# Full 128x128 stationary operands for the attention of a fused LayerNorm, attention and routed-FFN kernel on eight cores

## The reference

```python
mask = (ki <= qi) & ((qi - ki < WINDOW) | (ki < PERSIST))      # 128, 16
attn = softmax(where(mask, q @ k.T * hd**-0.5, min))
x + (attn @ v) @ Wo + ffn(xn)
```

## Time and profile before

| what | value |
|---|---|
| median of 3 runs | 5688.84 us |
| lowest and highest of the 3 | 5360.26 and 5897.46 us |
| the profiled execution | 5357.17 us |
| its span, slowest core | 5355.5 us |
| spans of the eight cores | 5347.5 to 5355.5 us |
| granted TensorE clock, mean of each core | 0.996 to 0.998 |
| PE busy, of the span | 98% |
| DVE, ACT, POOL busy | 28%, 20%, 5% |
| first scores, start of periods 0 and 7 | 3745.3 and 5161.7 us |

### The profile page before, as it was taken

One profiled execution on the slowest core, in us unless ns is written; L12 is line 12 of the kernel. 1 busy time (PEld: TensorE's weight loads), 2 busy tenths in 40 slices (PEclk: granted clock), 3 DMA queues, 4 the chain that ended last, 5 costly groups with the idle time before them and its releaser, 6 DMA issues.

```text
span 5355.5 us, 77837 instructions; the slowest of 8 cores (5347.5 to 5355.5 us)
## 1 busy us (share of the span) xinstructions
PE 5274.2 (98%) x27655; PEld 2478.0 (46%) x27655; DVE 1498.3 (28%) x3547; ACT 1083.1 (20%) x2801; POOL 253.4 (5%) x369
## 2 busy tenths in 40 slices
PE   6999999999999999999999999999999999999998
PEld 3444444444444444444444444444444444444444
DVE  3201013310111431102123010112555445454454
ACT  3010110101001010010100101001544344344343
POOL 1111011000000000000000000000000000000000
PEclk9999999999999999999999999999999999999999
DMA  9777779733342753343272222236254563654546
GB/s 224 152 152 151 172 157 225 192 97 90 90 110 79 236 130 98 99 99 103 93 253 79 79 79 71 72 126 228 95 170 134 168 191 115 183 179 134 165 135 196
DMA packets 255857, 749.90 MB, mean 140 GB/s; under 512 B 20416, under 2 KB 109056, under 8 KB 248320
## 3 DMA queue, kind: packets, MB, share of 16 engines
q1 hardware_dynamic: 130784, 482.74, 27.0%
q0 software_dynamic: 117984, 216.04, 20.4%
q10 hardware_dynamic: 6720, 46.14, 2.7%
HBM read 684.03 MB, written 174.06 MB: 160 GB/s over the span
## 4 chain that ended last, share of the span: by engine, by line
PE 96%; DMA 2%; issue 1%; DVE 0%; ACT 0%; SPq 0%; POOL 0%; ACTq 0%; DVEq 0%; POOLq 0%
PE ps L453 33%; PE ps L467 32%; PE ps L487 11%; PE ps L512 8%; PE ps L502 2%; PE ps L495 2%; PE ps L565 1%; PE ps L547 1%; PE ps L568 1%; DMA ring<-w 1%; DMA ring<-wt 1%; PE ps L545 1%; DMA acc<-x 1%; PE ps L546 1%; PE ps L532 1%
## 5 line engine op out<-in xcount | busy, mean ns | idle before, releaser
L453 PE MATMUL ps<-xnT,ring 128*128 128x512 bf16 x8192 | 1779.9, 380 | 11.1 <-DMA ring<-wt 5.7
L467 PE MATMUL ps<-ring,hT 128*128 128x512 bf16 x8192 | 1777.6, 379 | 4.5 <-DMA ring<-w 4.5
L453 PEld LDWEIGHTS ps<-xnT,ring 128*128 128x128 bf16 x8192 | 802.5, 98 | 982.3 <-issue 22.4
L467 PEld LDWEIGHTS ps<-ring,hT 128*128 128x128 bf16 x8192 | 801.0, 98 | 968.0 <-issue 9.3
L681 DVE SCALAR_TENSOR_TENSOR acc<-ps,gcol,acc 128x512 f32<-128x512 f32 x512 | 384.2, 750 | 2627.6 <-PE ps L467 2627.3
L832 ACT ACTIVATE hT<-ps,b1T 128x512 bf16<-128x512 f32 x512 | 351.7, 687 | 3113.8 <-PE ps L453 3113.0
L487 PE MATMUL ps<-xnT,ring 128*128 128x512 bf16 x2560 | 591.0, 380 | 0.1
L512 PE MATMUL ps<-ring,qT 128*128 128x512 bf16 x2048 | 478.1, 382 | 2.4 <-DMA ring<-wt 2.4
L932 ACT COPY pT_sb<-ps 128x384 bf16<-128x384 bf16 x512 | 244.6, 478 | 658.3 <-PE ps L547 646.9
L487 PEld LDWEIGHTS ps<-xnT,ring 128*128 128x128 bf16 x2560 | 232.6, 98 | 265.0 <-issue 0.2
L924 ACT ACTIVATE p_sb<-ps,negmax 128x272 bf16<-128x272 f32 x512 | 252.5, 493 | 218.1 <-DVE negmax L759 218.0
(11 more groups left out here) (82 smaller groups left out, 2435.4 us busy)
## 6 DMA issues: line engine op xcount, KB each, us to landing
ring<-wt SPq DMA_DIRECT2D x752, 512.0 KB, 5.6
ring<-w POOLq DMA_DIRECT2D x128, 512.0 KB, 12.8
wt<-ring SPq DMA_DIRECT2D x128, 512.0 KB, 6.9
acc_d<-acc POOLq DMA_DIRECT2D x16, 2048.0 KB, 16.6
base<-acc_d POOLq DMA_DIRECT2D x64, 512.0 KB, 10.7
y<-base POOLq DMA_DIRECT2D x64, 512.0 KB, 9.4
xln<-x ACTq DMA_DIRECT2D x24, 1024.0 KB, 9.2
acc<-x POOLq DMA_DIRECT2D x12, 2048.0 KB, 22.8
```

The lines of the kernel that those rows point to most:

```text
L453: i = e.matmul(bank(g)[:], w[:, cc, jj * 128:(jj + 1) * 128], xnT2[:, half, c, :], start=(c == 0), stop=(c == 15))
L467: i = e.matmul(bank(g)[:], hT[:, c, s * 128:(s + 1) * 128], w[:, cc, :], start=(c == 0), stop=(c == 15))
```

## The change

All stationary operands of the attention become 128x128.

- `p_sb` grows from 272 to 384 columns; DVE writes zeros to columns 256 to 383 of its four buffers at the program's start (four memsets, counted by `v_set`), and the exponent and the normalisation still write the columns up to 271. The third transpose takes columns 256 to 383.
- `vper` grows from 16 to 128 rows. POOL fills both buffers with zeros before the attention stage, and `persist` waits for that (`g_zero`) and writes its 16 rows. The third values product takes all 128 rows.
- The two scores matmuls of 128 moving columns become one of 256 where the slots `a` and `b` lie next to each other in `kbuf` (five of six cases).
- For t = 0 the part before and the first keys are left out, and for t = 1 the first keys: in scores, transposes, values products, and in the columns that `mask`, `row_max`, `exponent`, `normalize` and `copy_pT` touch.
- The memsets of `kbuf` and `vbuf` on POOL, the memset of `ps_p` on DVE, and the waits of PE on them are gone.

```diff
...
     rinv = [A("rinv%d" % j, [128, 1], F32, o + 8480 + 32 * j) for j in range(4)]
-    p_sb = [A("p_sb%d" % j, [128, 272], BF16, o + 8608 + 576 * j) for j in range(4)]
-    pT_sb = [A("pT_sb%d" % j, [128, 384], BF16, o + 10912 + 768 * j) for j in range(2)]
-    stg_bf = A("stg_bf", [16, 128], BF16, o + 12448)
-    stg_f32 = A("stg_f32", [64, 128], F32, o + 12704)
-    o += 13248
+    p_sb = [A("p_sb%d" % j, [128, 384], BF16, o + 8608 + 768 * j) for j in range(4)]
+    pT_sb = [A("pT_sb%d" % j, [128, 384], BF16, o + 11680 + 768 * j) for j in range(2)]
+    stg_bf = A("stg_bf", [16, 128], BF16, o + 13216)
+    stg_f32 = A("stg_f32", [64, 128], F32, o + 13472)
+    o += 14016
...
     qT = [A("qT0", [128, H, BLK], BF16, o_ln), A("qT1", [128, H, BLK], BF16, o_acc)]
-    vper = [A("vper%d" % j, [16, Dm], BF16, o_ln + 16384 + 4096 * j) for j in range(2)]
+    vper = [A("vper%d" % j, [128, Dm], BF16, o_ln + 16384 + 4096 * j) for j in range(2)]
     vbuf = A("vbuf", [128, KS, Dm], BF16, o_acc + 16384)
...
     d_id, d_b1, d_mask, d_small = sem("d_id"), sem("d_b1"), sem("d_mask"), sem("d_small")
-    v_set, v_zero, g_zero = sem("v_set"), sem("v_zero"), sem("g_zero")
+    v_set, g_zero = sem("v_set"), sem("g_zero")
...
         return n % KS
+
+    def window(it):
+
+        t = it // NIT % BPB * NS + it % NIT // H
+        return t >= 1, t >= 2
+
+    def columns(it):
+        back, first = window(it)
+        return slice(0 if back else 128, 272 if first else 256)
...
                 wait_ffn_evicted(e, 4 + b2)
-                e.wait_ge(g_zero, 1)
+            back, first = window(it)
             q = qT[m % 2][:, h, s * 128:(s + 1) * 128]
             a, b = slot_k(m * NS + s + KS - 1), slot_k(m * NS + s)
-            e.matmul(ps_s[b2][:, 0:128], q, kbuf[:, a, h, :], start=True, stop=True)
-            e.matmul(ps_s[b2][:, 128:256], q, kbuf[:, b, h, :], start=True, stop=True)
-            e.matmul(ps_s[b2][:, 256:272], q, kper[m // BPB][:, h, :],
-                     start=True, stop=True).then_inc(t_sc, 1)
+            ps = ps_s[b2]
+            if back and a < b:
+                i = e.matmul(ps[:, 0:256].rearrange("p (s n) -> p s n", n=128), q,
+                             kbuf[:, a:b + 1, h, :], start=True, stop=True)
+            else:
+                if back:
+                    e.matmul(ps[:, 0:128], q, kbuf[:, a, h, :], start=True, stop=True)
+                i = e.matmul(ps[:, 128:256], q, kbuf[:, b, h, :], start=True, stop=True)
+            if first:
+                i = e.matmul(ps[:, 256:272], q, kper[m // BPB][:, h, :],
+                             start=True, stop=True)
+            i.then_inc(t_sc, 1)
...
             else:
-                e.wait_ge(v_zero, 1)
+                wait_ffn_evicted(e, 6)
+            back, first = window(it)
             pT = as_bf(ps_p)
-            e.transpose(pT[:, 0:128], p_sb[b4][:, 0:128], id_bf[:])
-            e.transpose(pT[:, 128:256], p_sb[b4][:, 128:256], id_bf[:])
-            e.transpose(pT[0:16, 256:384], p_sb[b4][:, 256:272],
-                        id_bf[:]).then_inc(t_pT, 1)
+            for c in [0] * back + [1] + [2] * first:
+                i = e.transpose(pT[:, c * 128:(c + 1) * 128],
+                                p_sb[b4][:, c * 128:(c + 1) * 128], id_bf[:])
+            i.then_inc(t_pT, 1)
...
                 wait_ffn_evicted(e, 7)
-                e.wait_ge(g_zero, 2)
+            back, first = window(it)
             p = pT_sb[it % 2]
-            a, b = slot_k(m * NS + s + KS - 1), slot_k(m * NS + s)
             hs = slice(h * 128, (h + 1) * 128)
-            e.matmul(ps_o[:, 0:128], vbuf[:, a, hs], p[:, 0:128], start=True, stop=False)
-            e.matmul(ps_o[:, 0:128], vbuf[:, b, hs], p[:, 128:256],
-                     start=False, stop=False)
-            e.matmul(ps_o[:, 0:128], vper[m // BPB][:, hs], p[0:16, 256:384],
-                     start=False, stop=True).then_inc(t_av, 1)
+            keys = [vbuf[:, slot_k(m * NS + s + KS - 1), hs], vbuf[:, slot_k(m * NS + s), hs],
+                    vper[m // BPB][:, hs]]
+            seen = [0] * back + [1] + [2] * first
+            for c in seen:
+                i = e.matmul(ps_o[:, 0:128], keys[c], p[:, c * 128:(c + 1) * 128],
+                             start=(c == seen[0]), stop=(c == seen[-1]))
+            i.then_inc(t_av, 1)
...
         e.memset(mhalf[:], -0.5).then_inc(v_set, 1)
+        for j in range(4):
+            e.memset(p_sb[j][:, 256:384], 0.0).then_inc(v_set, 1)
         n_bn = 0
...
             wait_evicted(e, ("v", b * BPB, 3, NS - 1))
-            e.tensor_copy(vper[b][:], vbuf[0:PER, sk, :]).then_inc(v_per, 1)
+            e.wait_ge(g_zero, 2)
+            e.tensor_copy(vper[b][0:PER, :], vbuf[0:PER, sk, :]).then_inc(v_per, 1)
         def mask(it):
             m, s = it // NIT, it % NIT // H
             t = (m % BPB) * NS + s
+            cols = columns(it)
             ps = ps_s[it % 2]
             e.wait_ge(t_sc, it + 1)
-            e.tensor_tensor(ps[:, 0:272], ps[:, 0:272], masks_sb[:, min(t, 2), :],
+            e.tensor_tensor(ps[:, cols], ps[:, cols], masks_sb[:, min(t, 2), cols],
                             ALU.add).then_inc(v_msk, 1)
         def row_max(it):
             e.wait_ge(v_msk, it + 1)
-            e.reduce_max(negmax[it % 4][:], ps_s[it % 2][:, 0:272], axis=AX.X,
+            e.reduce_max(negmax[it % 4][:], ps_s[it % 2][:, columns(it)], axis=AX.X,
                          negate=True).then_inc(v_max, 1)
...
             e.wait_ge(v_inv, it + 1)
-            e.tensor_scalar(p_sb[b4][:], p_sb[b4][:], rinv[b4][:], None,
-                            ALU.mult).then_inc(v_p, 1)
-
-        wait_ffn_evicted(e, 6)
-        e.memset(ps_p[:, 128:192], 0.0).then_inc(v_zero, 1)
+            p = p_sb[b4][:, columns(it)]
+            e.tensor_scalar(p, p, rinv[b4][:], None, ALU.mult).then_inc(v_p, 1)
+
         e.wait_ge(d_mask, 48)
...
                 e.wait_ge(t_pT, it - 3)
-            e.activation(out=p_sb[b4][:], in_=ps_s[it % 2][:, 0:272], func=AF.Exp,
+            cols = columns(it)
+            if it < 4:
+                e.wait_ge(v_set, 6)
+            e.activation(out=p_sb[b4][:, cols], in_=ps_s[it % 2][:, cols], func=AF.Exp,
                          bias=negmax[b4][:],
...
                 e.wait_ge(t_av, it - 1)
-            e.copy(pT_sb[it % 2][:], as_bf(ps_p)[:, 0:384]).then_inc(a_pT, 1)
+            back, first = window(it)
+            cols = slice(0 if back else 128, 384 if first else 256)
+            e.copy(pT_sb[it % 2][:, cols], as_bf(ps_p)[:, cols]).then_inc(a_pT, 1)
...
-        e.wait_ge(t_d, P.ffn_units)
-        e.memset(kbuf[:, KS - 1, :, :], 0.0).then_inc(g_zero, 1)
+        for b in range(BPC):
+            e.memset(vper[b][:], 0.0).then_inc(g_zero, 1)
         for sl in range(4):
             e.wait_ge(st_acc[sl], 16 * NFB)
-        e.memset(vbuf[:, KS - 1, :], 0.0).then_inc(g_zero, 1)
```

## The result

Against the kernel before, on the same chips, the ratio of times is 0.9626, with an interval of 0.961 to 0.9642: 3.7% faster. The changed kernel's median of 5 runs is 5160.9 us, the shortest 5153.65; the profiled execution takes 5159.94. The shortest of before is 5358.29. Some executions of either kernel are longer since the cores of one die or of both are granted a lower clock (in the changed kernel's 5950.69 us, cores 4 to 7 have 0.852 to 0.857 where cores 0 to 3 have 0.995 to 0.998, and in a later execution of the kernel before, of 5820.25 us, 0.912 to 0.915); the ratios leave them out, but medians of few runs are moved by them, so that 5688.84 against 5160.9 isn't what the change did.

A forecast was written before the change was run, and what follows sets the result against it. PE was taken as the bound, busy for 98% of the span. Savings of 202 + 1 + 14 less 11 and 8 gave 198, taken as 200 us: 5157 us from 5357.17, 8-in-10 range 5130 to 5217.

The forecast's parts named there:

- Part 1: Attention slots: third transpose and third values product full size, small steps 0.056 us each; saves 0.394 us per slot, 202 us.
- The bound of 0.07 for a full step: Transposes and values products: largest step seen between two full operands, putting the six between 0.33 and 0.42 us.
- Part 2: Scores: one product of 256 columns takes 0.109 us against 0.112 for two of 128; saves 1 us in all.
- Part 3: Items with t = 0 and t = 1: skipped parts save 10 us and 4.5 us, together 14 us.
- Part 4: Gains given back as PE waits: 11 us for the probabilities in short slots, 8 us for key banks.
- key banks: Slots with three key units: ACT evicts after its copy of the transposed probabilities, so PE waits for banks; 8 us lost.
- Part 5: Moved memsets on POOL and DVE, loads of `base`, and PE's new wait for the bank of `ps_p`: costed at nothing.
- One padding alone: Rival: only one of the two paddings helps, part 1 gives 96 us less; 5241 us, 6%.
- Had the size not been the cause: Rival: operand size doesn't cause the long steps, they stay and only the skips gain, 38 us; 5319 us, 3%.
- The slots of 8 matmuls: Rival: the probabilities' way bounds these slots, 2.40 us instead of 2.21, giving back 60 us; 5217 us, 6%.
- The slower rival: PE's waits bring the clock to 1.2 GHz in periods 0, 4 and 7, costing 409 us; 5566 us, 2%.
- The step that failed: Whole execution: 5157 us forecast against the profiled 5357.17; the same ratio on the median of 5688.84 would be 5476.

The follow-up runs named there:

- e1: The changed kernel with the third values product back at 16 rows, only the third transpose full size; 5236 us.
- e2: The changed kernel with the third transpose back at 16 columns, only the third values product full size; 5233 us.
- e5: The kernel before, with the 16-column transpose made twice and the 16-row values product made twice, first in its group; 5354 to 5358 us on cores 0 to 3.
- e6: The changed kernel with the third transpose at w columns and third values product at w rows; 5159.5 us with 120, 5326.4 us with 64.
- e3: The changed kernel with the scores always in two products of 128 columns; spans of 5148 to 5155 us on cores 4 to 7.
- e4: The changed kernel without skipped parts, all three done for each item, memsets of `kbuf` and `vbuf` back; 5173.9 us.
- e9: The changed kernel with dense matmuls dealt one by one in periods 0 and 7, and key and value units alternating; 5147.1 us, ratio 0.9607.
- e10: The changed kernel with dense matmuls dealt one by one in periods 0 and 7, and ACT evicting ahead of both copies in a slot; 5128.1 us, ratio 0.9571.

## Where the prediction was right, and where not

The forecast was 5157 us for an execution like the profiled one; measured were 5159.94, 5153.65 and 5160.9, ratio 0.9626 against the forecast 0.963. The mechanism held, part by part, and one step failed: how the sum was turned into a time beside the median (last bullet).

- **Part 1** (0.394 us per slot, 202 us): a slot's small work fell from 0.87 to 0.47, that is 0.40 us, 0.06 from start to start through transposes, values and the step to the dense work. That the long steps stand where the form changes is shown by e1 and e2 (0.20 us per slot each), by e5 (no long step behind an operand of the same form, the same in each direction) and by e6. That what is exposed there is the load, as the prediction puts it, is not shown: in the earlier trace rows and in e1 the load's row starts together with its matmul's or 0.01 before, so the extra 0.09 lies ahead of both, and may be a pause ahead of the load rather than the load itself. The prediction holds the 0.15 on each side against the rule of the Trainium skill (TensorE: Matmul & The Clock Gate, LDWEIGHTS (loading the stationary operand)) on a load's time, but 0.15 is a step and not a load's length; the lengths are given at e1. The bound of 0.07 for a full step wasn't needed: full operands behind full ones are 0.055 apart (4631.65 to 4631.76 for two), and the step of 0.07 after `vbuf`'s first product stands only behind a partial operand.
- **Part 2** (1 us): the merged product took the interpolated 0.11, and e3 shows no difference. The strided read costs nothing that shows.
- **Part 3** (14 us): 13.6, from e4.
- **Part 4** (11 us for the probabilities, 8 for key banks): the waits grew by 11.2 and 8.7 us. That the first fits so well is in part luck: slot by slot the sizes were off, and the loss is more than these rows show. Period 7 was to take about 127 us and took 130.9. Two slots without dense work in it, core 0:

```profile
4988.02 0.27 PE L543 MATMUL ps<-kbuf,qT 128*128 128x256 bf16 x1
...
4988.36 0.69 DVE L759 TENSOR_TENSOR base<-ps,base 128x512 f32<-128x512 f32 x1 [0.82 <-PE ps L521]
...
4989.91 0.33 PE L564 MATMUL ps<-id_bf_sb,p_sb 128*128 128x128 bf16 x3 [1.14 <-DVE p_sb L793]
...
4996.61 0.27 PE L543 MATMUL ps<-kbuf,qT 128*128 128x256 bf16 x1
...
4998.23 0.33 PE L564 MATMUL ps<-id_bf_sb,p_sb 128*128 128x128 bf16 x3 [0.67 <-DVE p_sb L793]
```

The first kind is as worked out up to the transposes: 4988.02 to 4989.91 is 1.89 us, as in the earlier trace rows, and the 0.40 gained is all wait; its dense work then starts up to 0.2 us later than elsewhere, for a reason that the trace doesn't name. The second kind, where DVE has nothing to evict in between, was never held to 1.89: the transposes came 1.33 us after its start in the kernel before, and 1.62 here, and the wait grew from 0.2 to 0.67. The scores behind it come some 0.2 later, when the exponent of two items before ends, and the values product waits some 0.07 for ACT's copy. Over the 16 slots the loss is 0.6 each and not 0.40, some 4 us more than worked out. What made up for it on core 0 are the 4.1 us from the last slot on, which no part of the prediction has. For the key units the size was right (8.7 against 8), and so was the mechanism as the prediction put it, ACT's copy ahead of the evictions: e9, which took the three evictions in a row for the cause, fell, and e10, which took away their place behind the copy, ended the waits.
- **Part 5** (nothing): the first scores start at 3745.6 against 3745.3 on core 0.
- **The other rivals.** One padding alone was priced at 5241 us; e1 and e2, which have one each, took 5236 and 5233. Had the size not been the cause, it would have been 5319. The slots of 8 matmuls take 2.20 us (4631.35 to 4633.55) and don't wait.
- **The slower rival** needed the clock to fall; it is 1.00 in all periods, also where PE waits 14 us in period 7.
- **The step that failed** is the last one, from the sum to a time beside the median of the kernel before. The prediction said that the other two of the three runs are longer "by something that the profile doesn't show", gave this no price, and named 5157 us with 5688.84 standing as the time before. That is 532 us or 9.3% less. The parts of the sum account for 200 of them; the other 332 (5688.84 less 5357.17) are that something. What the runs showed in its place: the change is worth 3.7%, 197 us between the two profiled executions (5357.17 to 5159.94), and the 332 us are no part of it, since the lower granted clock that the section on the result tells of meets both kernels (for the three runs themselves no clock is on record). The figure that the prediction gave for the median, 5476, didn't come either, since the median after is 5160.9. It is partly luck that 5157 stands so near to the measured times: core 0's attention saved 203.7 us, 3.7 more than the sum, and the later start of the core that is slowest now took 6.5 of them back.

## What to carry to other kernels

When many small matmuls stand among large ones, read the steps from start to start, and look for stationary operands whose form differs from their neighbours'. Padding one with zeros cost nothing here, where the moving side stays the same, and won 0.20 us each time. Putting partial ones of one form side by side may save part of it; e5 shows this for the same operand used twice. When the bound engine gets faster in slots of a fixed schedule, list the slots that become shorter than the side chain, and deal its work so that none is; then see what stands idle in front of ready work in another engine's order.

## What the runs showed of the hardware

- Behind an operand of the same form, a load starts 0.05 to 0.06 us before its own matmul, beside the one that is running. At a change of form it starts with its matmul or 0.01 before, and the step between the matmuls is 0.14 to 0.16 us instead of 0.06. The step is 0.06 to 0.07 where a partial operand is used twice (e5), and as long between two different partial forms (0.15) as between full and partial.
- The length of a load's row says little about this: 98 ns for 128x128, 90 for 16x128 and 85 for 128x16 in the kernel before. With 128x120 it is 131 ns (e6), and hidden all the same.
- Operands of 120 rows or columns stream like full ones (0.06, 5159.5 us in all); with 64 the steps are those of 16 (0.16 behind 64 rows, 5326.4 us in all).
- A moving operand of two runs of 128 columns, whose starts are 4 KB apart, takes 0.11 us, no more than two products of 128 columns (e3).
